# One head's two query tiles as a pair in a banded attention loop, three turned blocks per pair, and the first norm in eight steps

## What is computed

```python
W = 64                                     # window; d = 16, NH = 12, S = 256
kp = jnp.pad(k, ((0,0),(0,0),(W,W),(0,0)))
idx = jnp.arange(S // W)[:, None] * W + jnp.arange(3 * W)[None, :]
kb, vb = kp[:, :, idx], vp[:, :, idx]
scores = jnp.einsum('bhcqd,bhckd->bhcqk', qc, kb) / jnp.sqrt(d)
allowed = in_mask & inside_sequence & (abs(key - query) <= W)
scores = jnp.where(allowed, scores, -1e9)
out = jnp.einsum('bhcqk,bhckd->bhcqd', jax.nn.softmax(scores, -1), vb)
h = layer_norm(h + out @ Wo + bo, ln1_s, ln1_b)
f = gelu(h @ W1 + b1);  h = layer_norm(h + f @ W2 + b2, ln2_s, ln2_b)
```

## Time and profile before

| what | value |
|---|---|
| median of three runs | 1976.86 us (1970.09 to 1981.36) |
| profiled execution | 1966.12 us, span 1964.3 us, mean granted TensorE clock 0.898 |
| busy of the span | PE 1532.7 us (78%), weight loads 1290.7, DVE 1340.6 (68%), ACT 1026.9 (52%), POOL 712.5 (36%) |
| first to last score maximum, banded loops 1 to 4 | 80.4 to 238.5, 351.5 to 508.2, 621.2 to 777.7, 887.3 to 1040.9 us |
| the same of the unbanded loop | 1480.4 to 1628.9 us |

### The profile page before, as it was taken

How to read it: one execution, slowest core, us unless ns; L and a number is a source line. 1 busy time by engine, 2 the same in 40 slices (tenths; PEclk the granted TensorE clock), 3 DMA queues, 4 the chain that set the end, 5 groups by cost and what they waited for, 6 DMA issues and landing times.

```text
span 1964.3 us, 45857 instructions
## 1 busy us (share of the span) xinstructions
PE 1532.7 (78%) x14634; PEld 1290.7 (66%) x14634; DVE 1340.6 (68%) x3638; ACT 1026.9 (52%) x2392; POOL 712.5 (36%) x993
## 2 busy tenths in 40 slices
PE   0689889789798898898897938849818886669992
PEld 0467668677677776786776827729816664569992
DVE  4698966789876989668997662253358998344444
ACT  0478733688534787337884313225417883235661
POOL 5554123553134641236531320024525421045541
PEclk9899989899898999899998968769958997679996
DMA  5645101634004451016430000046526430067775
GB/s 130 185 108 115 28 1 31 163 76 87 1 2 128 85 116 28 1 32 160 88 74 1 1 13 1 1 142 189 168 72 140 85 63 23 22 200 241 239 219 173
DMA packets 144329, 178.46 MB, mean 91 GB/s; under 512 B 22096, under 2 KB 106128, under 8 KB 143952
## 3 DMA queue, kind: packets, MB, share of 16 engines
q1 hardware_dynamic: 136784, 158.18, 31.6%
q0 software_dynamic: 7296, 17.18, 2.6%
HBM read 132.96 MB, written 42.34 MB: 89 GB/s over the span
## 4 chain that ended last, share of the span: by engine, by line
PE 31%; DVE 14%; issue 4%; ACT 2%; DMA 2%; POOL 1%; SPq 0%; DVEq 0%; ACTq 0%; POOLq 0%
PE bank L1414 7%; DVE ptl L772 4%; DVE neg_max L766 2%; PE bank L1400 2%; PE bank L548 2%; PE bank L618 2%; DVE xn L886 1%; PE bank L1403 1%; DMA xn<-y_rows 1%; PE bank L1401 1%; PE bank L1402 1%; PE bank L1404 1%; PE bank L423 1%; PE bank L1158 1%; ACT pth L670 1%
## 5 line engine op out<-in xcount | busy, mean ns | idle before, releaser
L660 ACT ACTIVATE prob<-bank,neg_max 128x192 f32<-128x192 f32 (+1 forms) x960 | 408.1, 436 | 132.2 <-DVE neg_max L766 79.0
L772 DVE TENSOR_TENSOR ptl<-bank,pth 128x512 f16<-128x512 f32 x480 | 327.0, 681 | 11.8 <-ACT pth L670 5.6
L766 DVE TENSOR_REDUCE neg_max<-bank 128x2 f32<-128x384 f32 (+1 forms) x480 | 273.4, 570 | 77.5 <-PE bank L537 68.7
L548 PE MATMUL bank<-ident,prob 128*128 128x128 f32 x1920 | 309.6, 285 | 0.0
L670 ACT ACTIVATE pth<-bank 128x512 f16<-128x512 f32 x480 | 284.8, 593 | 7.8 <-PE bank L548 7.5
L566 PE MATMUL bank<-v,pth 128*128 128x33 bf16 x1920 | 200.8, 181 | 106.7 <-DVE ptl L772 89.6
L566 PEld LDWEIGHTS bank<-v,pth 128*128 128x128 f16 x1920 | 154.7, 96 | 190.5 <-DVE ptl L772 177.5
L625 ACT ACTIVATE xx<-bank 128x256 fp32r<-128x256 f32 x256 | 95.7, 387 | 239.8 <-PE bank L423 235.6
L548 PEld LDWEIGHTS bank<-ident,prob 128*128 128x128 f32 x1920 | 205.1, 142 | 0.1
L568 PE MATMUL bank<-v,ptl 128*128 128x33 bf16 x1920 | 194.9, 177 | 0.0
L567 PE MATMUL bank<-v,pth 128*128 128x16 bf16 x1920 | 191.0, 170 | 1.9 <-issue 1.9
(11 more groups left out here) (281 smaller groups left out, 4078.7 us busy)
## 6 DMA issues: line engine op xcount, KB each, us to landing
xn<-in_e_seg SPq DMA_DIRECT2D x34, 768.0 KB, 6.7
w<-in_e_w SPq DMA_DIRECT2D x23, 576.0 KB, 4.2
qk_rows<-fbuf SPq DMA_DIRECT2D x128, 96.0 KB, 2.3
qx<-qk_rows SPq DMA_DIRECT2D x35, 288.0 KB, 4.1
kx<-qk_rows SPq DMA_DIRECT2D x35, 288.0 KB, 5.7
qk_rows<-w SPq DMA_DIRECT2D x80, 96.0 KB, 2.3
qx<-qk_rows SPq DMA_DIRECT2D x35, 192.0 KB, 4.7
kx<-qk_rows SPq DMA_DIRECT2D x35, 192.0 KB, 5.5
```

Source lines behind the costliest of these rows:

```text
L548: last = nc.tensor.transpose(bank[BT[p % 2]][:, (2 * e + c) * P:(2 * e + c) * P + P], prob[:, qt, hd % PROBS, c * P:c * P + P], ident[:, :])
L660: nc.scalar.activation(prob[:, qt, hd % PROBS, c0:c0 + n], scores_at(u // 2, n)[:, u % 2, :], ACT.Exp, bias=neg_max[:, tile_no % 3, hd:hd ...
L766: nc.vector.tensor_reduce(neg_max[:, t % 3, hd:hd + 2], scores_at(p, D if banded else S), AX.X, ALU.max, negate=True).then_inc(max_ready.s ...
L772: nc.vector.tensor_tensor(ptl[:, p % 2, :], bank[BT[p % 2]][:, :], pth[:, p % 3, :], ALU.subtract)\
```

## The change

Pairs are formed otherwise: a pair is now one head with both query tiles of its sequence. `where(u)` gives the query tile from the lowest bit. `prob` becomes a ring `probs` of six pairs, in which the banded loop writes the 192 keys of the first tile and right behind them the 192 of the second, 384 columns in all. These are three blocks of 128: keys 0 to 127 for tile 0; keys 128 to 191 for tile 0 and, below them, keys 64 to 127 for tile 1; keys 128 to 255 for tile 1. So the banded loop turns three blocks, and the value products for the middle block use rows 0 to 63 of it for the first tile and rows 64 to 127 for the second. The unbanded loop keeps four blocks and full rows. The value products are split in two halves of six with the turn between them; the banded halves wait for each other. The finish handles six heads with both tiles in place of one tile with twelve heads. The norm of the first group is done in eight steps at p = 94 to 101 by the function that does the last group's, generalised.

```diff
-            return u // (2 * HEADS), u // HEADS % 2, u % HEADS
+            return u // (2 * HEADS), u % 2, u // 2 % HEADS
...
+        probs = flat(prob[:, :, :, :], "p a s n -> p (a s n)").rearrange("p (r n) -> p r n", r=PROBS)
...
-        pad_ready = sig("pad_ready", per=NT)
+        pad_ready = sig("pad_ready", per=B)
-        pv_done = sig("pv_done", per=PAIRS)
+        pv_done, first_half = sig("pv_done", per=PAIRS), sig("first_tile_values_done", per=PAIRS)
...
             if banded:
-                nc.tensor.matmul(o, ident_bf, mask[:, 2 * b + qt, :].unsqueeze(1).to_broadcast([P, 2, D]),
-                                 start=True, stop=False)
-            for e in range(2):
-                last = nc.tensor.matmul(o[:, e, :], qx[0:ROWS, b % 3, hd + e, qt * P:qt * P + P],
-                                        kx[0:ROWS, b % 3, hd + e, ks], start=not banded, stop=e == 1 or not banded)
+                nc.tensor.matmul(o, ident_bf, mask[:, 2 * b:2 * b + 2, :], start=True, stop=False)
+            for qt in range(2):
+                last = nc.tensor.matmul(o[:, qt, :], qx[0:ROWS, b % 3, hd, qt * P:qt * P + P],
+                                        kx[0:ROWS, b % 3, hd, keys(qt, banded)], start=not banded,
+                                        stop=qt == 1 or not banded)
...
+        def turns(banded):
+            return 3 if banded else 4
...
-            for e in range(2):
-                _, qt, hd = where(2 * p + e)
-                for c in range(2):
-                    last = nc.tensor.transpose(bank[BT[p % 2]][:, (2 * e + c) * P:(2 * e + c) * P + P],
-                                               prob[:, qt, hd % PROBS, c * P:c * P + P], ident[:, :])
+            for c in range(turns(banded)):
+                last = nc.tensor.transpose(bank[BT[p % 2]][:, c * P:c * P + P], probs[:, p % PROBS, c * P:c * P + P],
+                                           ident[:, :])
...
+        def pe_values(pe, it, p, banded, qt):
+
+            b, _, hd = where(2 * p)
+            if qt == 0:
+                pe.wait_ge(lo_ready.sem, lo_ready.at(it, p + 1))
+                pe.wait_ge(v3_ready.sem, v3_ready.at(it, 4 * (b // 2) + 2 * (b % 2) + 2))
+                if p % 6 == 0:
+                    pe.wait_ge(att_ready.sem, att_ready.at(it, p // 6 - 1))
+            if banded:
+                pe.wait_ge((first_half if qt else pv_done).sem, (first_half if qt else pv_done).at(it, p + qt))
+            o = bank[BV[p // 6 % 2]]
+            every_row = slice(0, P)
+            if banded:
+                parts = ((0, 0, every_row), (1, 1, slice(0, P - WIN))) if qt == 0 else \
+                    ((2, 1, every_row), (1, 0, slice(P - WIN, P)))
+            else:
+                parts = ((2 * qt, 0, every_row), (2 * qt + 1, 1, every_row))
+            for i, (turn, chunk, rows) in enumerate(parts):
+                w, v = slice(turn * P, turn * P + P), v3[rows, (b // 2) % 2, 2 * (b % 2) + chunk, hd, :]
+                c = (hd % 6 * 2 + qt) * OC
+                o2, o1 = o[:, c:c + OC], o[:, c + 1 + DH:c + OC]
+                nc.tensor.matmul(o2, pth[rows, p % 3, w], v[:, 0:OC], start=i == 0, stop=False)
+                nc.tensor.matmul(o1, pth[rows, p % 3, w], v[:, OC:VC], start=False, stop=False)
+                last = nc.tensor.matmul(o2, ptl[rows, p % 2, w], v[:, 0:OC], start=False, stop=i == 1)
+            last.then_inc((pv_done if qt else first_half).sem, 1)
...
                 if p >= 5:
-                    pe_values(pe, it, p - 5)
+                    pe_values(pe, it, p - 5, banded, 0)
...
                 if 0 <= p - 3 < PAIRS:
-                    pe_turn_probs(pe, it, p - 3)
+                    pe_turn_probs(pe, it, p - 3, banded)
+                if p >= 5:
+                    pe_values(pe, it, p - 5, banded, 1)
                 pe_step(pe, it, p, banded, w, w_out, tile, xx)
...
-            act.wait_ge(max_ready.sem, max_ready.at(it, u // 2 + 1))
-            back = u - PROBS if hd >= PROBS else u - 2 * HEADS + PROBS
-            if back >= 0:
-                act.wait_ge(t_done.sem, t_done.at(it, back // 2 + 1))
+            act.wait_ge(max_ready.sem, max_ready.at(it, p + 1))
+            if qt == 0 and p >= PROBS:
+                act.wait_ge(t_done.sem, t_done.at(it, p - PROBS + 1))
...
-            nc.scalar.activation(pth[:, p % 3, :], bank[BT[p % 2]][:, :], ACT.Copy).then_inc(hi_ready.sem, 1)
+            n = turns(banded) * P
+            nc.scalar.activation(pth[:, p % 3, 0:n], bank[BT[p % 2]][:, 0:n], ACT.Copy).then_inc(hi_ready.sem, 1)
...
-            nc.vector.tensor_tensor(ptl[:, p % 2, :], bank[BT[p % 2]][:, :], pth[:, p % 3, :], ALU.subtract)\
+            n = turns(banded) * P
+            nc.vector.tensor_tensor(ptl[:, p % 2, 0:n], bank[BT[p % 2]][:, 0:n], pth[:, p % 3, 0:n], ALU.subtract)\
                 .then_inc(lo_ready.sem, 1)
...
-            if banded and p == PAIRS + 2:
-                dve.wait_ge(rows_y.sem, rows_y.at(it, 16 * 8))
-                dve_affine(dve, ch, it, NORMED.index((1, 0)) + 1, 0, 0)
+            if banded:
+                dve_norm_step(dve, ch, it, p - LATE[2 * GT - 1] - 10, NORMED.index((1, 0)) + 1, 0, 0)
...
                 if banded:
-                    finish_marks[0] = ch.mark(nc.vector.scalar_tensor_tensor(
-                        rs2[:, 0, :], in0=pad_exp[:, r3, :], scalar=pad_keys[:, t % 2:t % 2 + 1],
-                        in1=po[:, :, 0], op0=ALU.mult, op1=ALU.add))
+                    for qt in range(2):
+                        finish_marks[0] = ch.mark(nc.vector.scalar_tensor_tensor(
+                            by_tile(rs2[:, 0, :])[:, :, qt], in0=by_tile(pad_exp[:, b % 2, :])[:, heads, qt],
+                            scalar=pad_keys[:, qt:qt + 1], in1=by_tile(po[:, :, 0])[:, :, qt], op0=ALU.mult, op1=ALU.add))
...
-                nc.vector.tensor_tensor(o[:, 0:HEADS, :], au[:, :, :], r, ALU.mult)
-                nc.vector.tensor_tensor(o[:, HEADS:, :], au[:, 8:HEADS, :], r[:, 8:HEADS, :], ALU.mult)\
-                    .then_inc(att_ready.sem, 1)
+                last = nc.vector.tensor_tensor(o[:, :, heads, :], x, r, ALU.mult)
+                if half:
+                    last = nc.vector.tensor_tensor(o[:, :, HEADS:, :], x[:, :, 2:6, :], r[:, :, 2:6, :], ALU.mult)
+                last.then_inc(att_ready.sem, 1)
...
-                pe_transpose(pe, it, turned(1, a), a, xn, att_ready, it, a + 1, True)
+                pe_transpose(pe, it, turned(1, a), a, xn, att_ready, it, a // 2 * 2 + 2, True)
...
-            nc.gpsimd.memset(neg_half[:, :], -0.5)
-            nc.gpsimd.memset(prob[:, 0, :, D:2 * P], 0.0)
-            nc.gpsimd.memset(prob[:, 1, :, 0:WIN], 0.0).then_inc(zeroed.sem, 1)
+            nc.gpsimd.memset(neg_half[:, :], -0.5).then_inc(zeroed.sem, 1)
```

More of the change, by code:

```diff
@@ L432, in pe_turn @@
                 if k == 1:
-                    pe_transpose(pe, it, turned(k, t), t, xn, att_ready, it, t + 1)
+                    pe_transpose(pe, it, turned(k, t), t, xn, att_ready, it, t // 2 * 2 + 2)
                 else:
@@ L524, in pe_scores @@
         def pe_scores(pe, it, p, banded):
-            b, qt, hd = where(2 * p)
+            b, _, hd = where(2 * p)
             pe.wait_ge(exp_done.sem, exp_done.at(it, 2 * p - 4))
-            if b == 0 and qt == 0 and hd % 4 == 0:
+            if b == 0 and hd % 4 == 0:
                 pe.wait_ge(first_in[hd // 4].sem, first_in[hd // 4].at(it, 16 * READS))
-            elif b and p % (PAIRS // B) == 0:
+            elif hd == 0:
                 pe.wait_ge(qk_in[b % 3].sem, qk_in[b % 3].at(it, 16 * READS * (b // 3 + (b % 3 > 0))))
-            ks = keys(qt, banded)
@@ L544, in pe_turn_probs @@
             pe.wait_ge(exp_done.sem, exp_done.at(it, 2 * p + 2))
-            for e in range(2):
-                _, qt, hd = where(2 * p + e)
-                for c in range(2):
-                    last = nc.tensor.transpose(bank[BT[p % 2]][:, (2 * e + c) * P:(2 * e + c) * P + P],
-                                               prob[:, qt, hd % PROBS, c * P:c * P + P], ident[:, :])
-            last.then_inc(t_done.sem, 1)
-        def pe_values(pe, it, p):
-            b, qt, _ = where(2 * p)
-            pe.wait_ge(lo_ready.sem, lo_ready.at(it, p + 1))
-            pe.wait_ge(v3_ready.sem, v3_ready.at(it, 4 * (b // 2) + 2 * (b % 2) + 2))
-            if p % 6 == 0:
-                pe.wait_ge(att_ready.sem, att_ready.at(it, 2 * b + qt - 1))
-            for e in range(2):
-                hd = (2 * p + e) % HEADS
-                o = bank[BV[qt]]
-                for c in range(2):
-                    w = slice((2 * e + c) * P, (2 * e + c) * P + P)
-                    v = v3[:, (b // 2) % 2, 2 * (b % 2) + c, hd, :]
-                    o2, o1 = o[:, hd * OC:hd * OC + OC], o[:, hd * OC + 1 + DH:hd * OC + OC]
-                    nc.tensor.matmul(o2, pth[:, p % 3, w], v[:, 0:OC], start=(c == 0), stop=False)
```

(17 more changed lines are left out.)

72 lines of the change are left out of this document (38 added, 34 removed).

## The result

The changed kernel took **2103.45 us**, median of four runs (2072.21 to 2152.56), beside 1974.64 (1970.09 to 1981.36) for the kernel before: 1.0547 times as long, 95% interval 1.0437 to 1.0658. The profiled execution took 2112.53 us, span 2110.7, mean granted clock 0.828 in place of 0.898.

What follows compares the result with a forecast made beforehand. No engine was full: a ring of engines with little slack bound the loops, and PE would become the bound. Banded pairs +35, norm steps -6, unbanded loop -2 gave +27 us on 1976.86: 2004 us, range 1925 to 2070.

Steps and rivals of the forecast that it cites:

- The clock falls: Rival: PE stands in drains, a fifth of each banded loop goes slow; +69 us more, about 2073; chance 0.05.
- (d): Sum per banded pair: PE becomes longest, most waits go, 0.06 kept; 1.735 us against 1.645, +35 us.
- the dearest switch alone: Upper bound of the tile switch in banded pairs: 0.155 us each, 1.915 a pair, 2073 us.
- (f): Unbanded loop 2 us less (0 to 5); pad exponential once per batch on twice the elements; last turn's wait under 1 us.
- (a): Three turned blocks in banded loops: per pair PE -0.11, DVE -0.13, ACT -0.11 us; finish +0.02.
- (b): Middle block in halves: four 64/128-row tile switches a banded pair, 0.11 us each, 0.44 a pair; bounds 0 and 0.155.
- the smaller rival: Rival: a tile switch costs about 0.09 us, no weight load showing; -4 - 8, 1973 us; chance 0.20.
- The two fp32 places: Tile switches in the old trace, in the router and at 512 columns: 0.10 and 0.09 us each.
- (c): PE's added waits on itself: nothing under cover of turns or scores, 0.18 us each without.
- (e): First norm in eight steps fills idle time at the loop's end: 1.5 us a layer, 6 in all; bounds 0 and 14.
- no switch cost: Rival: two-byte matmuls pay no tile switch, all three engines shed 0.11 us a pair; -50, 1927 us; chance 0.17.
- The waits do not go: Rival: PE's waits for ptl stay at 0.30 us a banded pair; pair 1.975, 2096 us; chance 0.08.

Runs made afterwards that it cites:

- Number 2: The changed kernel with the mask product issued twice per banded pair, the first overwritten; 2047 us, 1.037 of the kernel before.
- number 6: The changed kernel with the pad exponential after every six heads in place of once per batch; 2028 us, 2029 when run again.
- 10: The changed kernel with 128 rows in the middle block, all value products in a row before the turn, two uncovered self-waits; 2095 us.
- number 1: The changed kernel with all 128 rows in the middle block's value products, so no tile switches; 1939 us, 0.982 of the kernel before.
- 9: The changed kernel with value products ordered full, half, half, full and the turn behind, two tile switches a pair for four; 2247 us.
- number 7: The changed kernel with 128 rows in the middle block and the pad exponential after every six heads; 1915 us, 0.975 of the kernel before.
- number 8: The changed kernel with 128-row products on a zero-padded block-diagonal value copy, no self-wait, pad exponential after every six heads; 1936 us.

## Why the prediction was wrong

**The step that failed is the clock.** "The clock falls" was a rival with a chance of 0.05 and a price of 69 us on top of the forecast, by which a fifth of each loop would be slow. It was 347 of 772 us, 45%, and cost 105. The rival's own sentence, that PE stands in drains where it stood in waits, was the right mechanism; its chance was set as if a full engine could not lose its clock. In the sum of (d) the clock stood only inside the 0.06 a pair kept for all waits, 23 us over the four loops. Number 2 (more work, 56 us faster), 6 (one wait less, 75 us) and 10 (the clock falls without any half tile) show it. The range ended at 2070, about where this rival alone (2073) or the dearest switch alone (2073) would have put it, so it had no room for a clock lost for longer than a fifth.

**The second is in (f): the pad exponential "once per batch on twice the elements"** was costed by its work and not by who waits for it. Its due time moved from six pairs ahead of the first half's finish to the same step of the program. At full clock that is some 10 us; with the clock, 75 and 107 between the medians of the two comparisons, 50 and 79 between the fastest executions.

The rest of the sum held. At the clock of before the profiled execution would have taken some 2008 us, against a forecast for it of 1966 + 27 = 1993; 10 of the 15 us between are the pad wait.

- (a) DVE's low halves are 547 ns, its maximum 550 (0.55 taken for both), ACT's copy 486. DVE has 1.33 us a pair by the window (1.35 forecast), ACT 1.23 (1.21).
- (b) 0.095 (against number 1) to 0.0975 a switch, where 0.11 was taken and 0.09 was the smaller rival. PE's pair without a wait is 1.39 + 0.235 = 1.625, not 1.675. The two fp32 places, read as 0.10 and 0.09, told the price of a two-byte switch within a hundredth: the share of the weight load that I added was not there. The windows promised 163 to 168 us; number 6's third loop has 162, at 0.98.
- (c) Covered self-waits cost nothing seen (1), uncovered ones 0.21 where 0.18 was said (9, 10).
- (d) The waits went nearly as said; pairs at full clock took 1.70 to 1.73, forecast 1.735.
- (e) -10, forecast -6, inside its bounds. DVE's norm steps wait for no `rstd`.
- (f) The unbanded loop took 1.8 us less, forecast 2 less.
- Rivals: "no switch cost" gave 50 us less than before, and number 7 measured 52. "The waits do not go" fell: those for `ptl` went from 11.5 to 4.9 us, though "nearly vanish" said more.

**What stays open.** Why the clock comes back after 3.4 to 6.8 us in the kernel before and in number 1, and mostly only after 31 to 106 us in the change. The runs only show what makes the stretches fewer and shorter. The one at the second dozen of pairs, which number 6 still has, comes at a place that all these kernels share. PE's row just before the fall at 389.5 in number 6 (for 34.1 us), then the one just before the fall at 645.0 in the kernel before (for 3.4 us):

```profile
389.29 0.19 PE L576 MATMUL bank<-v,pth 128*128 128x33 bf16 x1 [0.93 <-DVE ptl L782]
```

```profile
644.57 0.19 PE L566 MATMUL bank<-v,pth 128*128 128x33 bf16 x1 [1.32 <-DVE ptl L772]
```

In number 6 DVE then has, one behind the other from 386.29 to 388.69, a tile's low part, a piece of the last group's norm, the first finish of the loop and a maximum. That this crowd starts the stretch was not tested.

## What to carry to other kernels

When a change makes TensorE the bound by switches, self-waits or other standing time and not by streamed work, as this one did, price the clock with it: read the granted clock for each loop, and count a microsecond at half clock by two windows of the same work at different clocks (0.34 here). Small waits elsewhere can then matter far above their own length, so for every signal that a change gives less often, ask which consumer used to find it long done. And a half-filled block was better met by padded operands over the whole tile (number 8, 1936 us) than by alternating tiles (number 6, 2028).

## What was not expected of the hardware

- One microsecond in which PE stood, behind a wait of 0.92 us on DVE, was followed by 105.8 us at 1.2 GHz, with PE's records covering 97% of them; the same program's third loop had 31 us of it at once. Busy time by records did not tell whether the clock was kept. The Trainium skill (TensorE: Matmul & The Clock Gate, A second HAM failure mode: psum-queue depth-cycling) describes a clock that swings through short idle times between groups of products; these loops agree in that the clock fell while PE stood only for a microsecond at a time; they differ in that it stayed down, for 105.8 us here.
- Added work made the kernel faster: 384 useless mask products, 56 us less by the medians.
- At half clock the step across a tile switch was 0.12 us, at full clock 0.11.
- A wait of PE on its own last product cost 0.21 us in the open (numbers 9 and 10), twice a switch, whether the tile changes or not.
